# Layer 2 self-attention of a four-layer decoder: another order of the same steps on TensorE, VectorE, ScalarE and GpSimd

## The reference

```python
qkv = jnp.einsum('bsd,dhf->bshf', x, w_qkv) + b_qkv        # f = 192
q, k, v = jnp.split(qkv, 3, axis=-1)
q = q * cos + _rotate_half(q) * sin
k = k * cos + _rotate_half(k) * sin
scores = jnp.einsum('bhqd,bhkd->bhqk', q, k) / jnp.sqrt(jnp.float32(f))
alibi = rel[None, :, :] * slopes[:, None, None] * MAX_BIAS  # rel = min(key - query, 0)
scores = jnp.where(causal == 0, -1000000000.0, scores + alibi[None])
weights = jax.nn.softmax(scores, axis=-1)
attn = jnp.einsum('bhqk,bhkd->bhqd', weights, v)
return jnp.einsum('bshd,hdm->bsm', attn, w_out) + b_out
```

## Time and profile before

| what | us |
|---|---|
| median of 3 runs | 3091.52 (3089.79 to 3096.44) |
| the profiled execution, its own time | 3087.09 |
| its span | 3085.0 |
| busy in the span: TensorE matmuls / VectorE / ScalarE / GpSimd | 2376.2 / 1795.4 / 1270.8 / 631.3 |
| mean granted clock of TensorE over the span | 0.87 of full speed |

### The profile page before, as it was taken

One profiled execution on the slowest core, in us unless ns is written; L12 is line 12 of the kernel. 1 busy time (PEld: TensorE's weight loads), 2 busy tenths in 40 slices (PEclk: granted clock), 3 DMA queues, 4 the chain that ended last, 5 costly groups with the idle time before them and its releaser, 6 DMA issues. The chain is left out here.

```text
span 3085.0 us, 40803 instructions
## 1 busy us (share of the span) xinstructions
PE 2376.2 (77%) x12384; PEld 1405.9 (46%) x12384; DVE 1795.4 (58%) x4355; ACT 1270.8 (41%) x2637; POOL 631.3 (20%) x583
## 2 busy tenths in 40 slices
PE   6864886668598888797788888676888789578487
PEld 4653651236423332564444444463444355557454
DVE  4665349979566555445444444346666634635777
ACT  3442346534354444222666666434444422123212
POOL 0410005534200000001555555431000000044100
PEclk7885987969699999798999999887999889688799
DMA  0000000010100000001222221100000000100000
GB/s 32 32 6 0 1 5 0 1 45 1 56 1 0 0 0 0 1 0 58 70 69 69 69 69 52 43 1 25 1 0 0 0 0 0 62 19 1 1 0 14
DMA packets 19881, 61.86 MB, mean 20 GB/s; under 512 B 4928, under 2 KB 4928, under 8 KB 18592
## 3 DMA queue, kind: packets, MB, share of 16 engines
q1 hardware_dynamic: 19488, 59.53, 6.1%
q10 hardware_dynamic: 256, 0.68, 0.1%
HBM read 42.37 MB, written 1.05 MB: 14 GB/s over the span
## 5 line engine op out<-in xcount | busy, mean ns | idle before, releaser
L824 ACT ACTIVATE PT<-P 128x512 f32<-128x512 f32 (+3 forms) x512 | 244.0, 516 | 231.9 <-PE P L496 122.1
L689 DVE TENSOR_REDUCE MF<-P 128x1 f32<-128x512 f32 (+3 forms) x512 | 281.7, 586 | 97.5 <-PE P L479 53.0
L2450 PE MATMUL P<-XT,W 128*128 x424 | 221.0, 617 | 63.4 <-ACTq L2484 63.4
L2526 DVE SCALAR_TENSOR_TENSOR X<-P,WE,X 128x128 f32 x576 | 162.2, 344 | 166.2 <-PE P L2467 161.6
L2467 PEld LDWEIGHTS P<-W,e_h 128*128 128x128 f32 (+1 forms) x1952 | 220.3, 190 | 61.0 <-issue 56.8
L2467 PE MATMUL P<-W,e_h 128*128 128x128 f32 (+1 forms) x1952 | 227.5, 277 | 3.4 <-DVE X L2526 3.4
L1286 POOL TENSOR_TENSOR d_e<-d_e,d_rc 128x512 f32<-128x512 f32 (+3 forms) x256 | 178.2, 723 | 219.2 <-DVE d_rc L1193 219.1
L2495 ACT ACTIVATE e_g<-P 128x512 f32<-128x512 f32 x148 | 88.4, 597 | 311.9 <-PE P L2450 311.9
L479 PE MATMUL P<-KA,QA 128*128 128x512 bf16 (+3 forms) x512 | 184.2, 366 | 25.5 <-ACT KA L808 15.1
L496 PE MATMUL P<-QA,KA 128*128 128x512 bf16 (+3 forms) x512 | 178.1, 354 | 32.3 <-ACT PT L824 12.7
L541 PE MATMUL P<-PT,VA 128*32 128x512 f32 (+3 forms) x1024 | 195.8, 518 | 0.0
(11 more groups left out here) (357 smaller groups left out, 4705.4 us busy)
## 6 DMA issues: line engine op xcount, KB each, us to landing
d_bt<-in_alibi SPq DMA_DIRECT2D x32, 512.0 KB, 3.6
d_moved<-d_raw SPq DMA_DIRECT2D x256, 64.0 KB, 2.0
W<-in_w_L_xattn SPq DMA_DIRECT2D x1, 4291.0 KB, 12.8
W<-in_w_L_ffn SPq DMA_DIRECT2D x1, 3333.0 KB, 11.3
W<-in_w_L_ffn SPq DMA_DIRECT2D x1, 3155.0 KB, 10.3
W<-in_w_L_attn SPq DMA_DIRECT2D x1, 2636.0 KB, 12.5
W<-in_w_L_ffn SPq DMA_DIRECT2D x1, 2310.0 KB, 8.9
W<-in_w_L_ffn SPq DMA_DIRECT2D x1, 1744.0 KB, 7.3
```

The lines of the kernel that those rows point to most:

```text
L689: last = v.tensor_reduce(col, src, AX.X, ALU.max, negate=True)
L824: a.activation(k.PT[0:self.kp, h % self.slots, t, N - w:N], src, ACT.Exp, scale=self.scale).then_inc(s("exp_done"), 1)
L2450: pe.matmul(P[:, PG + j % 2, :], w["w1"][:, col:col + 128], x, start=True, stop=True).then_inc(s("gate"), 1)
L2526: last = v.scalar_tensor_tensor(x, y, k.WE[:, bass.ds(c * 4 + t, 1), e], x, ALU.mult, ALU.add)
```

## The change

Four loops get another order; no step is changed, added or removed, and every wait stays with its step.

- TensorE: in each part, `scores` moves behind `values`, `result` and `weighted`, to the end of the part.
- VectorE: in each part, `recip` (of the part before) moves ahead of `biased`.
- ScalarE: in part 1, the copy of the values moves ahead of the exponentials.
- GpSimd: in parts 1 and 3, `rope` (the rotary sum) moves ahead of `shares` (of the part before).

```diff
--- before.py
+++ after.py
@@ -1145,14 +1145,14 @@
                         projected(n, j // 2)
                     if 0 <= n - 3 < ITEMS:
                         turn(n - 3, j)
-                    if 0 <= n - 2 < ITEMS:
-                        scores(n - 2, j)
                     if j == 1 and 0 <= n - 2 < ITEMS:
                         values(n - 2)
                     if j == 1 and 0 <= n - 5 < ITEMS:
                         result(n - 5)
                     if 0 <= n - 4 < ITEMS:
                         weighted(n - 4, j)
+                    if 0 <= n - 2 < ITEMS:
+                        scores(n - 2, j)
 
         @block.vector
         def _(v):
@@ -1205,12 +1205,12 @@
                         by_cos(n, j // 2)
                     if j % 2 == 0 and 0 <= n - 1 < ITEMS:
                         by_sin(n - 1, j // 2)
-                    if 0 <= n - 2 < ITEMS:
-                        biased(n - 2, j)
                     if j >= 1 and 0 <= n - 2 < ITEMS:
                         recip(n - 2, j - 1)
                     if j == 0 and 0 <= n - 3 < ITEMS:
                         recip(n - 3, QT - 1)
+                    if 0 <= n - 2 < ITEMS:
+                        biased(n - 2, j)
                     if j == 2 and n >= 5 and (n - 5) % PAIRS == PAIRS - 1 and n - 5 < ITEMS:
                         add((n - 5) // PAIRS)
 
@@ -1262,10 +1262,10 @@
                         outputs(n - 5)
                     if 0 <= n - 3 < ITEMS:
                         turned(n - 3, j)
+                    if j == 1 and 0 <= n - 2 < ITEMS:
+                        values(n - 2)
                     if 0 <= n - 2 < ITEMS:
                         exponentials(n - 2, j)
-                    if j == 1 and 0 <= n - 2 < ITEMS:
-                        values(n - 2)
 
         @block.gpsimd
         def _(g):
@@ -1288,12 +1288,12 @@
 
             for n in range(ITEMS + 3):
                 for j in range(QT):
+                    if j % 2 == 1 and 0 <= n - 1 < ITEMS:
+                        rope(n - 1, j // 2)
                     if j >= 1 and 0 <= n - 2 < ITEMS:
                         shares(n - 2, j - 1)
                     if j == 0 and 0 <= n - 3 < ITEMS:
                         shares(n - 3, QT - 1)
-                    if j % 2 == 1 and 0 <= n - 1 < ITEMS:
-                        rope(n - 1, j // 2)
 
 
 def merge_low_rank(k, i):
```

## The result

The changed kernel takes 3037.5 us (median of 4 runs, 3033.81 to 3039.77) against 3093.4 us before (4 runs, 3089.79 to 3096.44). The ratio is 0.9819 with a 95% interval of 0.9802 to 0.9836: 1.8% faster. The forecast was 3044 us in a range of 3032 to 3066. The profiled execution took 3036.1 us, its span is 3034.3.

A forecast was written before the change was run, and what follows sets the result against it. No engine is full; a closed chain through GpSimd's keys' sum sets 15.05 us an item. Shortened to 13.78, times 31 intervals, it saves 39.4 us, plus 7.9 of clock falls: 47.3 off 3091.5 gives 3044 us, range 3032 to 3066.

The forecast's parts named there:

- The old chain: Keys' projection, copy, products, reciprocal, GpSimd's shares, keys' sum, next scores: a closed loop of 15.05 us an item.
- The new chain: From scores 1 over ScalarE and VectorE (4.94 us), then TensorE alone (8.84): 13.78 us an item, saving 39.4 us.
- The spare of the other loops: Loops beside the chain have slack: 1.2 us at the keys' sum, 0.5 at part 3 and the queries' copy.
- The clock: Five falls of TensorE's clock to 1.2 GHz after the 1.75 us wait all go: -7.9 us, bounds -7.9 to 0.
- the prediction's signs: What would show it right, among others: items 13.8 us apart, keys' sum 1.27 us, granted clock 1.00 through the stage.
- Rival D: Clock falls in nearly every item at the wait for scores 3: 18 us slower, 3110 us; chance 0.06.
- The fill: Start of the stage, first items: counted at nothing, bounds -5 and +3 us.
- the range's low end: 3032 us: the forecast with the fill's 5 us and new-chain hand-overs shorter by 0.2 us an item (6 us).
- Rival B: VectorE and GpSimd's shared read path stretches the products on the new chain by 0.50 us: 14.28 us, 3060; chance 0.12.
- the 0.08 us said above: Part 0's transposes on TensorE: 1.04 us busy, less 0.08 in which the next group runs beside it, 0.96 counted.

The follow-up runs named there:

- e1: Kernel before with GpSimd's reorder alone (rotary sum ahead of shares): 13.42 us an item, 3035.9 us, ratio 0.9809.
- e8: Changed kernel with VectorE's cosine product last and TensorE's scores ahead of result and weighted sums, behind the value projection: 12.38 us an item, 2997.1 us.
- e9: Changed kernel with VectorE's cosine product last and TensorE's scores behind result but ahead of the weighted sums: 12.19 us an item, 2988.7 us.
- e11: Changed kernel with the queries' sine product done twice on VectorE (part 0, 0.61 us added): 13.53 us an item, 3037.2 us.
- e6: Changed kernel with TensorE's order undone (scores back behind the transposes): 13.52 us an item, 3035.6 us.
- e7: Changed kernel with VectorE in the order sine, reciprocal, biased, cosine product last: 12.71 us an item, 3007.0 us.
- e4: Changed kernel with GpSimd's order undone (shares ahead of the rotary sums): 13.62 us an item, 3040.1 us.
- e3: Changed kernel with VectorE's order undone (biased ahead of the reciprocal): 13.99 us an item, 3058.6 us.
- e10: Changed kernel with the keys' sine product done twice on VectorE (part 2, 0.61 us added): 14.13 us an item, 3066.4 us.
- e5: Changed kernel with ScalarE's order undone (values' copy behind part 1's exponentials): 15.34 to 16.61 us an item, 3115.8 us.
- e2: Kernel before with TensorE's reorder alone (scores last in each part): 16.41 us an item, 3140.2 us, ratio 1.0142.

## Why the prediction was right

*The old chain.* Right, and shown by e1: with the two things that I named taken out of it (1.18 us of shares, 0.50 of stretch) an item took 13.42 us for 13.37 worked out, and it still closed at the keys' sum.

*The new chain.* The right links, and a sum slightly too long: 13.78 forecast, 13.53 measured. The part on VectorE and ScalarE was 4.94 and is 4.89. `biased` 3 waits for the exponentials through its reciprocal, as forecast (0.88 us until 1712.74), off the chain. TensorE's part was 8.84 and is 8.65: I took the stretch from 1707.72 to 1714.21 "in another order" at its old length. In the new order the transposes of part 1 take 0.71 us (0.80 before, when scores followed) and the value projection 0.89 (1.00 when scores came ahead). That was the mis-sized term, 0.20 us an item, 6 us in all; e8 and e9 show the same difference with one group moved.

*The spare of the other loops.* The keys' sum was given 1.2 us to spare; it has 1.27. Part 0's products were given 0.5; e11 added 0.61 and the item did not get longer: what stands behind, `biased` 0, has time until scores 1, as the prediction has it.

*The clock.* The term was -7.9 us for "five falls that all go". There were six. The last that it names, at 1909.15, is the one at the end of the stage, in an item of 16.57 us; five more lie ahead of it, in the items from 1614.26, 1676.03, 1767.91, 1829.68 and 1846.31. The last two of these are neighbours, with a granted clock of 0.90 in each, and only one of them can be in my count. And two stay, where the prediction's signs had 1.00 through the stage. 6 x 1.58 less 2 x 1.64 gives 6.2 us. The row of the 0.9 us wait, by which I took none, does not settle it. Both falls come right after the two waits of part 3 (0.56 or 0.57, then 0.76 us). Here is the first of them (TensorE's timeline):

```profile
1575.02 0.51 PE L1117 MATMUL P<-d_kr,d_qr 64*128 64x128 f32 x4 [0.76 <-DVE d_mn L1185]
1575.46 2.08 PE L1092 MATMUL P<-XT,W 128*128 128x512 f32 x2
```

The queries' projection takes 2.08 us instead of 1.12, and as it lies on the chain now, the item is 1.64 us longer. The Trainium skill's rule on this (TensorE: Matmul & The Clock Gate, "A second HAM failure mode: psum-queue depth-cycling"), that frequent short idles make the clock go back and forth, agrees in kind; by it none of the 7.9 us would have come, and the trace shows most of it did. Over most runs the number of falls goes with how long TensorE stands in an item: none where it is 1.0 and 1.1 us (e1, e6) or 0.6 and less (e7 to e9), one or two at 1.3 (e4, changed, e11), five or six in the steady part at 1.8 to 2.6 (e3, e10, before). It is a count and no rule: e5, which stands 3.1 us, has a fall in 20 of 26 steady items, and e2, which stands 4.1, in every second. Rival D had falls in nearly every item, at the wait for scores 3. It did not come here; e5 comes near its time (3115.8 us, the rival had 3110), with the falls behind another wait, 2.55 us at the keys' projection.

*The fill.* Counted at nothing with bounds of -5 and +3. The first three items took 46.6 us before and 38.5 after, 3.5 us beyond what the shorter item gives. In the first of them the granted clock was 0.51 before and 0.76 after, so how much of the 3.5 us is the order and how much the clock is open.

The terms together: 31 x 1.52 = 47.1, clock 6.2, fill 3.5, 56.8 us from the first scores 0 to the last; measured 475.1 - 418.65 = 56.5. Forecast for the stage 47.3, so 9 us too little: the items 7.7, the fill 3.5, the clock 1.7 the other way. The items alone came further out than the 6 us that the range's low end allowed them; the time lies inside because the fill used only part of its 5 us and the clock gave back less. (Forecast, fill and 6 us make 3033, not 3032.)

*What each edit does.* Here the text was weaker than the sum. It listed what each reorder saves or costs as if all four were needed. That GpSimd's two lines alone would do, and the other three edits without them nearly as well (e4), that the scores' new place costs 1.4% on its own, and that in the changed kernel ScalarE's reorder keeps that off (e5), it did not say. The prediction weighed one chain for the whole change and never the chain of a part.

*Rival B* (GpSimd's work holds up the products) took place, off the chain. Changed kernel, part 0:

```profile
1700.54 1.18 POOL L1286 TENSOR_TENSOR d_e<-d_e,d_rc 128x256 f32<-128x256 f32 x2
...
1701.21 1.06 DVE L1167 TENSOR_TENSOR d_by_cos<-d_raw,W 128x512 f32<-128x512 f32 x1 [1.37 <-ACT d_raw L1242]
```

The cosine product is issued at 1701.21, while part 2's shares run until 1701.72, and takes 1.06 us instead of 0.69. This is what the Trainium skill (SBUF — State Buffer, on the shared port pair) says of any GpSimd instruction: who comes first keeps the pair for the whole instruction. The trace agrees: the product ends at 1702.27, 0.55 us after the shares. e11 shows that the place can bear it.

## What to carry to other kernels

When hand-ordered queues close into a chain, write down the chain of each edit by itself and not only of the whole change: here one of four edits gave everything by itself, the other three gave all but 0.09 us an item without it, and one of these was a loss that another covered. Then look in the new chain for a link that stands in a queue for no reason of data, as the sine product and `biased` behind the cosine product did; moving the cosine product gave another 30 us. Price a wait of TensorE with the clock fall that it may bring, not with its own length alone.

## What the runs showed of the hardware

- The length of a group of matmuls depends on its neighbours. From start to start, the value projection (8 matmuls of 128 columns) took 0.89 us between transposes and `result`, 0.98 with scores behind it and 1.00 with scores ahead; `result` 0.99 behind the value projection and 1.09 behind scores. The scores are the ones that use half of the rows (64 of 128). Beside the weighted sums and the keys' projection the same change shows no cost: with scores 1 put between them they took 0.79 and 0.96 us, as without. Why it costs 0.1 us elsewhere I did not test.
- A rotary sum or shares on GpSimd and a product on VectorE, all from tiles in SBUF, were held up by one another: 1.77 us instead of 1.27 for the sum when a product was ahead, 1.06 instead of 0.69 for the product when shares were ahead.
- A fall of the clock cost 1.58 us when it followed the wait for the keys' sum and 1.64 when it followed the wait for scores 3 (items of 16.63 for 15.05 and of 15.17 for 13.53 us).
- A group of matmuls starts before the profiled end of the one ahead by more than the 0.08 us said above: the earlier trace rows have 1714.21 + 1.13 against 1715.17, 0.17 us.
